# Second layer's loop of a four-layer kernel: an accumulating transfer for the last sum, inverse roots on ScalarE alone, the decay's product in row halves, and the row turn placed inside the gate's projection

## The reference, cut to what matters

```python
xw = xa + sx * (maa_w + mw);  xg = xa + sx * (maa_g + mg)      # and xk, xv, xr
w = exp(-exp(time_decay + tanh(xw @ decay_w1) @ decay_w2))      # decay
g = silu(xg @ Wg.T)                                             # gate
...                                                             # scan over time gives y
y = (y - gm) * rsqrt(gv + EPS) * gn_w + gn_b                    # per head
x = x + y * g @ Wo.T
xc = _ln(x, ln2_w, ln2_b)
sxc = concat([state row, xc[:, :-1]]) - xc
rr = sigmoid((xc + sxc * fmaa_r) @ fWr.T)
kk = square(relu((xc + sxc * fmaa_k) @ fWk.T))
x = x + rr * (kk @ fWv.T)
```

## Time and profile before

| | us |
|---|---|
| median of three executions | 3539.14 |
| profiled execution | 3535.91 |
| its span | 3534.1 |
| second layer's scans on DVE, first start to last | 1470.8 to 2244.9 |
| starts of `first` on PE in turns 1 to 6 | 1579.59, 1679.85, 1781.64, 1884.01, 1985.96, 2088.15 |

### The profile page before, as it was taken

How to read it: one execution, slowest core, us unless ns; L and a number is a source line. 1 busy time by engine, 2 the same in 40 slices (tenths; PEclk the granted TensorE clock), 3 DMA queues, 4 the chain that set the end, 5 groups by cost and what they waited for, 6 DMA issues and landing times. The chain is left out here.

```text
span 3534.1 us, 55156 instructions
## 1 busy us (share of the span) xinstructions
PE 3319.9 (94%) x21472; PEld 2547.0 (72%) x21472; DVE 2390.6 (68%) x3781; ACT 1787.9 (51%) x4255; POOL 196.2 (6%) x311
## 2 busy tenths in 40 slices
PE   7999999999999997889999998679999999699998
PEld 6777888887777785656666665357788788488885
DVE  6666666666665665499999999637777887642213
ACT  4555444444454443456565554427777777532222
POOL 0000000000000000000000000001111111000000
PEclk9999999999999999899999999879999999899999
DMA  5332212231122211544444444120001110210004
GB/s 215 124 105 107 108 72 76 97 115 72 72 96 90 78 73 57 156 114 103 111 108 102 114 103 108 41 108 3 35 31 70 44 48 31 88 53 24 24 12 162
DMA packets 93456, 296.08 MB, mean 84 GB/s; under 512 B 20016, under 2 KB 28208, under 8 KB 68752
## 3 DMA queue, kind: packets, MB, share of 16 engines
q1 hardware_dynamic: 64896, 186.47, 18.0%
q0 software_dynamic: 10368, 75.50, 5.6%
q10 hardware_dynamic: 17936, 30.59, 2.5%
HBM read 233.82 MB, written 58.72 MB: 83 GB/s over the span
## 5 line engine op out<-in xcount | busy, mean ns | idle before, releaser
L537 ACT ACTIVATE l_prob<-l_bank,l_nmax 128x512 f32<-128x512 f32 x512 | 345.3, 687 | 276.8 <-DVE l_nmax L679 276.8
L679 DVE TENSOR_REDUCE l_nmax<-l_bank 128x1 f32<-128x512 f32 x512 | 317.5, 682 | 71.4 <-PE l_bank L409 71.2
L375 PE MATMUL l_bank<-l_x_hi,l_w_hi 128*128 128x256 f32 x1024 | 298.0, 291 | 11.7 <-DVE l_x_lo L779 11.7
L702 DVE COPY l_probT<-l_bank 128x512 f32<-128x512 f32 x256 | 173.7, 689 | 175.3 <-PE l_bank L423 173.2
L375 PE MATMUL l_bank<-l_x_hi,l_w_lo 128*128 128x256 f32 x1024 | 290.9, 284 | 0.0
L375 PE MATMUL l_bank<-l_x_lo,l_w_hi 128*128 128x256 f32 x1024 | 290.7, 284 | 0.0
L1752 DVE TENSOR_TENSOR_SCAN l_kv<-l_wx,l_kv 128x2056 f32<-128x2056 f32 x64 | 283.8, 4434 | 1.6 <-DVE first_nrs L1765 1.2
L2320 ACT ACTIVATE l2a_sc<-l2a_sc,l2a_nmax 128x256 f32<-128x256 f32 x512 | 254.8, 508 | 41.1 <-DVE l2a_nmax L2436 41.1
L423 PE MATMUL l_bank<-l_ident,l_prob 128*128 128x128 f32 x2048 | 247.9, 275 | 10.7 <-DVE l_k_lo L695 6.3
L423 PEld LDWEIGHTS l_bank<-l_ident,l_prob 128*128 128x128 f32 x2048 | 225.8, 141 | 24.4 <-DVE l_k_lo L695 16.3
L445 PE MATMUL l_bank<-l_probT,l_v 128*64 128x512 f32 x1024 | 233.8, 598 | 0.0
(11 more groups left out here) (353 smaller groups left out, 8207.5 us busy)
## 6 DMA issues: line engine op xcount, KB each, us to landing
l_vb<-vd SPq DMA_DIRECT2D x64, 1024.0 KB
l_w_hi<-kept_w_hi POOLq DMA_DIRECT2D x24, 1024.0 KB, 8.2
l_w_lo<-kept_w_lo POOLq DMA_DIRECT2D x24, 1024.0 KB, 10.2
l_wv_hi<-kept_wv_hi POOLq DMA_DIRECT2D x12, 1024.0 KB, 5.1
l_wv_lo<-kept_wv_lo POOLq DMA_DIRECT2D x12, 1024.0 KB, 7.1
kept_w_hi<-l_w_hi SPq DMA_DIRECT2D x8, 1024.0 KB, 8.8
kept_w_lo<-l_w_lo SPq DMA_DIRECT2D x8, 1024.0 KB, 11.2
l2a_x<-x SPq DMA_DIRECT2D x16, 512.0 KB, 3.8
```

Of the source, the lines that this page charges most:

```text
L375: mm = pe.matmul(s.ap[:, c * ROWS:(c + 1) * ROWS], a[:, kt, c, g, :], b[:, kt, c * ROWS:(c + 1) * ROWS], start=m == 0, stop=m == 3 * KT - 1)
L537: act.activation(prob[h][:, it, :], s.ap[:, :], ACT.Exp, bias=nmax[:, n % 2, it, h:h + 1], accum_out=rsum[:, n % 2, it, h:h + 1]).then_inc ...
L679: dve.tensor_reduce(nmax[:, n % 2, it, h:h + 1], s.ap[:, :], AX.X, ALU.max, negate=True).then_inc(max_ready, 1)
L702: dve.tensor_copy(probT[0][:, j, :], s.ap[:, :]).then_inc(s.drained, 1)
```

## The change

Four edits, all in the second layer's loop.

1. The last sum. DVE no longer adds `xres` and the gated product. ACT writes `xres` to x2 early in the turn (before `stats_c`); DVE writes the gated product into `rv`, which is the memory of `sxc`; and POOL issues a transfer that adds it to x2 in memory. `shift_c` of the next turn waits for that transfer.
2. Inverse roots. ACT computes exp(-0.5 ln(v + eps)) in two activations in place of the square root; DVE's reciprocal goes.
3. The decay's product. `decay_w1` is doubled to 128 columns, so that tanh gives the same 64 rows twice, and `decay_w2` is laid out as two halves of 64 rows; `decay_out` alternates between row halves 0 to 63 and 64 to 127 of PE's array.
4. The row turn xc stands between the two halves of the gate's projection on PE and in the ring, not ahead of both.

```diff
         ring += [f"mw{p}_0", f"mw{p}_1"] if p is not None else []
+        ring += [f"g{p}_0"] if p is not None else []
         ring += [f"xc{c}_0", f"xc{c}_1"] if c is not None else []
-        ring += [f"g{p}_0", f"g{p}_1", f"mk{p}_0", f"mk{p}_1", f"d{p}"] if p is not None else []
+        ring += [f"g{p}_1", f"mk{p}_0", f"mk{p}_1", f"d{p}"] if p is not None else []
...
+                def add_out(c):
+                    pool.wait_ge(res_stored, 16 * (c + 1))
+                    pool.wait_ge(rv_ready, 2 * c + 2)
+                    pool.dma_start(x2[c].rearrange("(r p) n -> p r n", p=P), rv, accum_op=ALU.add).then_inc(out_added, 16)
...
                 def decay_out(p):
                     drained(pe, S[f"d{p}"])
                     for half in H2:
-                        s = S[f"w{p}_{half}"]
-                        free(pe, s)
-                        for ct in (2 * half, 2 * half + 1):
-                            mm = pe.matmul(s.ap[:, ct % 2 * ROWS:(ct % 2 + 1) * ROWS], w2b[0:64, ct * P:(ct + 1) * P], tT[0:64, 1, :],
+                        free(pe, S[f"w{p}_{half}"])
+                    for i in H2:
+                        for half in H2:
+                            s, own = S[f"w{p}_{half}"], slice(64 * half, 64 * half + 64)
+                            mm = pe.matmul(s.ap[:, i * ROWS:(i + 1) * ROWS], dw2[own, i * P:(i + 1) * P], tT[own, 1, :],
                                            start=True, stop=True)
-                        mm.then_inc(s.full, 1)
+                            if i == 1:
+                                mm.then_inc(s.full, 1)
...
+                    if 0 <= p < B:
+                        project(p, "g", (0,))
                     if c >= 0:
                         pe.wait_ge(cxn_ready, c + 1)
                         turn(f"xc{c}", tmp_rows)
                     if 0 <= p < B:
-                        project(p, "g")
+                        project(p, "g", (1,))
                         mixture(p, "k")
                         decay_in(p)
...
                 def roots(c):
-                    act.activation(rs[:, :], s.ap[:, 0:ROWS], ACT.Sqrt, bias=eps[:, 0:1]).then_inc(s.drained, 1)
+                    act.activation(rs[:, :], s.ap[:, 0:ROWS], ACT.Ln, bias=eps[:, 0:1]).then_inc(s.drained, 1)
+                    drained(act, s)
+                    act.activation(rs[:, :], rs[:, :], ACT.Exp, scale=-0.5).then_inc(rs_ready, 1)
...
-                def store(c):
-                    act.wait_ge(out_ready, c + 1)
-                    act.dma_start(x2[c].rearrange("(r p) n -> p r n", p=P), xres[:, :, :]).then_inc(out_stored, 16)
+                def store_res(c):
+                    for half in H2:
+                        drained(act, S[f"o{c}_{half}"])
+                    act.dma_start(x2[c].rearrange("(r p) n -> p r n", p=P), xres[:, :, :]).then_inc(res_stored, 16)
...
                     if c >= 0:
+                        store_res(c)
                         stats_c(c)
...
-                def inverse(c):
-                    drained(dve, S[f"var{c}"])
-                    dve.reciprocal(rs[:, :], rs[:, :]).then_inc(rs_ready, 1)
...
-                        dve.tensor_tensor(tmp_rows[:, half, :], s.ap[:, :], tmp_rows[:, half, :], ALU.mult).then_inc(rv_ready, 1)
+                        dve.tensor_tensor(rv[:, half, :], s.ap[:, :], tmp_rows[:, half, :], ALU.mult).then_inc(rv_ready, 1)
...
-                    dve.tensor_tensor(xres[:, :, :], xres[:, :, :], tmp_rows, ALU.add).then_inc(out_ready, 1)
```

More of the change, by code:

```diff
@@ L912, with l1_layer @@
 MIX = ["w", "k", "v", "r", "g"]
-def l1_layer(nc, first, d, att, x1, u, vd, x2):
+def l1_layer(nc, kept, first, d, att, x1, u, vd, x2):
     HS, NJ, PER, CG = 16, 8, 8, 32
@@ L966, in l1_layer @@
         w1, w2a, w2b = ph.sb("w1", [P, CT, 160]), ph.sb("w2a", [P, COLS]), ph.sb("w2b", [P, COLS])
-        dw1 = ph.sb("dw1", [P, CT, 64])
+        dw1, dw2 = ph.sb("dw1", [P, CT, P]), ph.sb("dw2", [P, ROWS])
         vec, vecc = ph.sb("vec", [P, 9, CT]), ph.sb("vecc", [P, 6, CT])
@@ L988, in l1_layer @@
         xc, sxc = ph.sb("xc", [P, CT, ROWS + 1]), ph.sb("sxc", [P, CT, ROWS])
+        rv = sxc[:, :, :].rearrange("p c t -> p (c t)").rearrange("p (r n) -> p r n", r=RT)
         zeroed, consts, wx_zeroed = ph.sem("zeroed"), ph.sem("consts"), ph.sem("wx_zeroed")
@@ L996, in l1_layer @@
         s0_in, vb_in = [ph.sem(f"s0_in{i}") for i in range(2)], [ph.sem(f"vb_in{i}") for i in range(NV)]
-        v_stored, out_stored = ph.sem("v_stored"), ph.sem("out_stored")
+        v_stored, res_stored = ph.sem("v_stored"), ph.sem("res_stored")
+        out_added = kept.enter_context(nc.semaphore("kept_out_added"))
         summed, dev_in, dev_ready = ph.sem("summed"), ph.sem("dev_in"), ph.sem("dev_ready")
@@ L1053, in load_res @@
                         sp.wait_ge(x1_stored, 16 * c)
-                        sp.wait_ge(out_stored, 16 * c)
+                        sp.wait_ge(res_stored, 16 * c)
                     sp.dma_start(xres[:, :, :], x1[c].rearrange("(r p) n -> p r n", p=P)).then_inc(res_in, 16)
@@ L1084, in _ @@
                 sp.dma_start(w2b[64:96, :], d["l1_w2"][P:160, :]).then_inc(w2_in, 16)
-                sp.dma_start(w2b[0:64, :], d["l1_dw2"]).then_inc(w2_in, 16)
+                sp.dma_start(dw2[:, :], d["l1_dw2"]).then_inc(w2_in, 16)
                 for n in ("Wv", "Wg"):
@@ L1130, in _ @@
                         deviations(sd, dev_in, dev_ready, b + 1)
+                    if b >= 1:
+                        add_out(b - 1)
+                pool.wait_ge(out_added, 16 * B)
             @block.tensor
@@ L1228, in decay_in @@
                     for kt in range(CT):
-                        mm = pe.matmul(s.ap[0:64, 0:ROWS], dw1[:, kt, :], xf[1][:, kt, :], start=kt == 0, stop=kt == CT - 1)
+                        mm = pe.matmul(s.ap[:, 0:ROWS], dw1[:, kt, :], xf[1][:, kt, :], start=kt == 0, stop=kt == CT - 1)
                     mm.then_inc(s.full, 1)
@@ L1528, in decay_in @@
                     full(act, S[f"mg{p}_1"])
-                    act.activation(tT[0:64, 1, :], s.ap[0:64, 0:ROWS], ACT.Tanh).then_inc(s.drained, 1)
+                    act.activation(tT[:, 1, :], s.ap[:, 0:ROWS], ACT.Tanh).then_inc(s.drained, 1)
                 def decay_out(p):
@@ L1852, in shift_c @@
                         full(dve, S[f"fr{c - 1}_1"])
+                        dve.wait_ge(out_added, 16 * c)
                     dve.tensor_tensor(sxc[:, :, :], xc[:, :, 0:ROWS], xc[:, :, 1:ROWS + 1], ALU.subtract).then_inc(sxc_ready, 1)
@@ L1881, in _ @@
                             first_input(p)
-                        if n == 1 and c >= 0:
-                            inverse(c)
                         if n == 2 and now:
@@ L3080, in program @@
         l0_attention(nc, kept, first, d, x, u, att, x1)
-        l1_layer(nc, first, d, att, x1, u, vd, x2)
+        l1_layer(nc, kept, first, d, att, x1, u, vd, x2)
         between_layers.close()
@@ L3114, in arrange @@
     d["l1_Wo"] = by_rows(w["Wo"].T[order])
-    d["l1_w1"], d["l1_dw1"] = by_rows(w["maa_w1"]), by_rows(w["decay_w1"])
-    d["l1_w2"], d["l1_dw2"] = w["maa_w2"].reshape(160, COLS), w["decay_w2"]
+    d["l1_w1"], d["l1_dw1"] = by_rows(w["maa_w1"]), by_rows(np.concatenate([w["decay_w1"], w["decay_w1"]], axis=1))
+    d["l1_w2"] = w["maa_w2"].reshape(160, COLS)
+    d["l1_dw2"] = np.concatenate([w["decay_w2"][:, :ROWS], w["decay_w2"][:, ROWS:]], axis=0)
     d["l1_vec"] = columns(w["ln1_w"], w["ln1_b"], w["maa_x"], *(w["maa_" + n] for n in MIX), w["time_decay"])
```

7 lines of the change are left out of this document (1 added, 6 removed).

## The result

The changed kernel takes 3576.55 us in the median of seven executions, the kernel before 3540.64; the ratio is 1.0100 with a 95% interval of 1.0086 to 1.0115. It is slower, as forecast, but by 36 us and not by 16, and above the range. Five of the seven lie between 3576.4 and 3579.7, the other two at 3557.3 and 3561.8.

The account below looks back on a forecast made before the run. PE, with a short detour over ACT and DVE, was taken to set the turn. +3.8 us a turn times five (+19), with -3.5 and +1 once, gave +16.5 and a forecast of 3555 us, range 3536 to 3574.

Parts of the forecast that it names:

- the two waits: New PE waits each turn: 2.2 us before first (0.39 before the change) and 3.2 before decay_in (none before).
- Inverse roots: Ahead of first_part on ACT: a second table load and activation add 1.8 us a turn; bounds 0.5 and 1.9.
- The row turn: On PE amid the gate: its wait goes, decay_in waits 3.2 us instead; net gain 0.5 us a turn.
- the prediction's lower-bound case: decay_in's wait on PE if DVE is ready at once for shift_c: 2.6 us.
- The decay's product: decay_out on PE in row halves, 1.99 us before: 0.9 us a turn gained, between nothing and 0.95.
- DVE's two instructions: Reciprocal and sum removed from DVE: 0 in turns 1 to 6, -3.5 us once from first of turn 6 on.
- The transfer: Accumulating transfer: 0 in the loop; at the layer's end +1 us once, with the sum's saving included.
- The clock: PE's clock falls: 1.7 us behind decay_in's wait, 0.85 at first's, 0.85 delaying the row turn, per turn.
- everything falls: Rival, chance 0.17: clock falls in full at three places (3.4, 1.7, 1.7 us), 7.2 a turn, 3572 us.

Follow-up runs that it names:

- roots_back: The changed kernel with square root on ACT and DVE's reciprocal as before, the rest as changed; 3560.1 us, ratio 1.0063 to the kernel before.
- no_exp_load: The changed kernel with Exp replaced by Copy, so no second table load stands ahead of first_part (head normalisation comes out otherwise); 3548.5 us, ratio 1.0031.
- bank_back: The changed kernel with the ring list of the kernel before, PE's order as changed; 3522.5 us, ratio 0.9962 to the kernel before.
- waits_filled: The changed kernel with products computed twice on PE ahead of both waits (decay_in's and first's), same result; 3554.6 us, ratio 1.0045.
- turn_alone: The kernel before with the fourth edit alone (row turn amid the gate, in PE's order and ring); 3560.3 us, ratio 1.0069.
- roots_later: bank_back with ACT's roots moved behind first_part; 3521.0 us, ratio 0.9957 to the kernel before.
- sums_earlier: roots_later with the one-column products (column_variances) ahead of project v on PE, not behind it; 3518.2 us, ratio 0.9941 to the kernel before.
- roots_alone: The kernel before with the second edit alone (inverse roots on ACT); 3542.8 us, ratio 1.0019.

## Why the prediction was wrong in size

The direction, the two waits and their causes were right; the step that failed is the sum's term for the clock, which took 3.4 us a turn where 7.4 came. The profiled execution is 40.6 us longer than the one before, against 16.5 in the sum: 24.1 short. Of these 17.0 lie in the five turns (36.0 against 19) and 7.3 behind them (4.8 against -3.5 + 1).

- *Inverse roots.* Put at +1.8 us a turn, `first`'s wait at 2.2. Right: measured 2.12 (0.39 before), with the load at 1.28 and Exp at 0.42 us. Shown by roots_back (0.39 again) and no_exp_load (0.85). The Trainium skill's rule of one load for ln and exp ("ScalarE: Activation LUTs", "Table sets: the hidden batching unit") doesn't hold for this build: the trace has both loads.
- *The row turn.* The wait ahead of it went. The one before `decay_in` was put at 3.2, within 2.6 to 4; measured 2.97, released by ACT's gate activation. The way there was partly another: I had DVE's `shift_c` set it, but DVE waits 2.94 us for ACT's turned rows, which was the prediction's lower-bound case. So the whole chain begins at the row turn on PE, and each us that slow products delay the turn is passed on to `decay_in`. Shown by bank_back, where the list of banks is all that differs.
- *The decay's product.* Put at -0.9; 1.99 to 1.13. Right.
- *DVE's two instructions.* Put at nothing in turns 1 to 6, and that was right: DVE idles 12 us a turn. Put at -3.5 once behind them; from `first` of turn 6 to the last scan's start it is 156.8 us before (2244.9 - 2088.15) and 157.2 after (2280.68 - 2123.46), so nothing was gained. In turn 6 DVE waits 3.39 us for ACT's mixture r, where it had no wait before; ACT comes to it in an unbroken run from PE's fk product, which stands behind `decay_in`'s wait on PE:

```profile
2193.94 1.23 DVE L1811 TENSOR_TENSOR l_xf<-l_xf,l_sx 128x1024 f32<-128x1024 f32 x1 [3.39 <-ACT l_xf L1525]
```

  With the bank mended the gain is there: 151.6 us in bank_back, 5.2 less than before.
- *The transfer.* In the loop it costs nothing, as put. At the end I took +1 with a landing of 5.4; it lands after 9.8 in the median of the eight, and the layer's last stretch grew by 2.9 us (5.0 to 7.9). Between the last scan's start and DVE's last product 1.5 us more have no cause shown.
- *The clock.* Here the sum fell short. I put 1.7 us behind `decay_in`'s wait, 0.85 before `first` and 0.85 ahead of the gate, 3.4 in all. Turn 3 shows (3.78 - 1.97) + (1.65 - 1.07) = 2.4, (2.95 - 1.97) + (2.57 - 1.91) = 1.6, and (3.64 - 1.99) + (1.94 - 1.07) + (4.48 - 3.62) = 3.4: together 7.4. Turns 2 to 5 are alike in this, and turn 1 lacks the fall behind `first`: 35.4 in five turns where I had 17. That is 18.4 short, a little more than the 17.0 that are missing there; the other terms come to 1.4 less than put. The error was twofold. I took two of the three falls as half chances, the one behind `first` on a single wait of 1.97 us that had none behind it; and the fall ahead of the gate, priced at 1.7 from turn 5 of the kernel before, costs 3.4 since it begins over mixture w already. The rival "everything falls" had 7.2 a turn, which is the mean that was measured, and 3572; but its parts were others (3.4 behind `decay_in`, 1.7 at each of the two other places, where 2.4, 1.6 and 3.4 came), and its -2.5 behind the turns didn't come, so it too met the number partly by luck.

That the sum had the right parts is shown by bank_back: its turns without any fall take 98.92 us, which is 96.8 us of PE's own work, 2.12 of waiting and nothing else. Two things stay open. One is what decides on the fall ahead of the gate: it costs 3.4 us in the changed kernel and in most turns of waits_filled, and nothing in turns 2 to 5 of turn_alone or 3 to 5 of bank_back. The other is why the executions of one program fall in two groups (3557 and 3562 against 3576 to 3580). The group near my forecast would be one in which fewer falls come, but only one of the seven was looked at in a trace, and none of the lower two.

## What to carry to other kernels

When a use is moved in a ring of buffers, ask not only what it now covers but whose reader its neighbours now wait for: with the same four edits, leaving the gate's bank where it had been made 3576.6 into 3522.5, faster than the kernel before (0.9962). How much of that the moved gate half brings by itself no run shows. Look at what stands ahead of a step on the engine that serves the busiest one: one more activation and one more table load ahead of `first_part` cost 1.73 us of wait in a turn, and the same load ahead of tanh cost nothing. And price a new wait on PE with the slow products behind it, in full: here the waits take 5.1 us a turn and the clock 7.4, where before they took 1.7 to 2.9 and 1.6 to 2.7 (turns 2 to 5).

## What was not expected of the hardware

PE can do more and the kernel be faster: with 24 products computed twice in each turn (5.4 us) the median went from 3576.6 to 3554.6. A row of light products can do what a wait does: sixteen records of one streamed column, a mixture over 32 rows and the picks were followed by the lower level without any idle time ahead (roots_later), and not in turns 1 to 5 once the one-column products stood amid dense ones (sums_earlier). It doesn't do so each time: bank_back has the same row in the same order, and in its turns 3 to 5 nothing slow follows. A wait of 2.12 us was followed by slow products each time in the changed kernel (turns 2 to 6), in roots_alone in every second turn, and in bank_back in two of six (3.65 and 3.52 us against 1.97): the same wait has no fixed price.
